# Weight preparation folded into an attention turn, the input fetched a turn earlier, tables for the edge turns, and zero-operand matmuls in TensorE's program

## The reference, cut to what matters

```
x -> attention   16 heads of width 8, twice: softmax(q k) v, and "lines" (exterior
                 products of w1,w2 with x, normalised) with geo_v; mixed by a gate
  -> FFN         activations and weights rounded to FP4 in blocks of 16, silu gate, 352 wide
  -> Mamba block RMS norm, 256 channels, causal conv of 4, 16 states scanned over 256 tokens
  -> FFN         512 wide, gelu; weights plus scale * outer products of tokens 1 to 16
```

## Time and profile before

| | us |
|---|---|
| median of 3 runs | 897.81 |
| the three runs | 893.03, 897.81, 901.17 |
| the profiled execution | 895.68 |
| its span, first to last instruction | 893.9 |
| PE busy, share of the span | 658.1, 74% |
| DVE busy | 626.8, 70% |
| ACT busy | 426.3, 48% |
| POOL busy | 350.5, 39% |
| mean granted TensorE clock | 0.859 |

### The profile page before, as it was taken

The page is one execution under the profiler, slowest core; times in us unless marked ns, Lnnn a source line. Parts: engine busy times, 40 slices in busy tenths (PEclk is TensorE's granted clock), DMA queues, the critical chain, the costliest instruction groups (busy, mean ns, idle before and its releaser), DMA issues.

```text
span 893.9 us, 12114 instructions
## 1 busy us (share of the span) xinstructions
PE 658.1 (74%) x3939; PEld 401.5 (45%) x3939; DVE 626.8 (70%) x1230; ACT 426.3 (48%) x896; POOL 350.5 (39%) x328
## 2 busy tenths in 40 slices
PE   3258763897769896898589858978698678866355
PEld 2134442554545464446444545546444454444124
DVE  1826167697868786887779785978698859754671
ACT  1212532682549344854377345825483438433522
POOL 5513131492219512653348223932184007300640
PEclk9995976898889968997889887997899879967695
DMA  5221300341034201430134003410242005000400
GB/s 135 72 76 44 104 9 28 113 161 47 1 122 141 89 0 50 165 136 0 48 120 182 1 19 126 152 54 0 74 168 104 0 16 167 24 1 6 164 25 7
DMA packets 40447, 65.99 MB, mean 74 GB/s; under 512 B 7281, under 2 KB 29634, under 8 KB 38082
## 3 DMA queue, kind: packets, MB, share of 16 engines
q1 hardware_dynamic: 38242, 64.57, 21.7%
q10 hardware_dynamic: 2176, 1.05, 0.4%
HBM read 57.68 MB, written 7.86 MB: 73 GB/s over the span
## 4 chain that ended last, share of the span: by engine, by line
PE 49%; DVE 31%; issue 9%; ACT 6%; DMA 3%; POOL 1%; SPq 0%; DVEq 0%; POOLq 0%
PE ps_s L1036 14%; PE ps_v L1036 10%; PE ps_f L1036 9%; PE ps_y L1036 7%; PE ps_n L1036 6%; DVE shared L997 5%; DVE mx L897 4%; DMA x_tm<-in_L_attn_x_dram 2%; DVE bn L821 1%; DVE x L834 1%; PE ps_f L1040 1%; DVE shared L1002 1%; DVE qamax L790 1%; ACT L602 1%; DVE z L942 1%
## 5 line engine op out<-in xcount | busy, mean ns | idle before, releaser
L581 POOL TENSOR_TENSOR shared<-u,bcrow 128x1024 f32<-128x1024 f32 x64 | 199.3, 3119 | 125.3 <-DVE u L986 79.9
L997 DVE TENSOR_TENSOR_SCAN shared<-ps_f,shared 128x512 f32<-128x512 f32 x128 | 151.6, 1212 | 26.9 <-POOL shared L581 15.5
L897 DVE TENSOR_REDUCE mx<-ps_s 128x2 f32<-128x512 f32 (+1 forms) x192 | 127.3, 686 | 55.5 <-PE ps_s L1036 54.6
L1036 PE MATMUL ps_s<-stack_mem 72*128 72x128 bf16 (+3 forms) x1024 | 152.7, 270 | 7.5 <-DVE mx L897 6.5
L1036 PE MATMUL ps_y<-shared,ident 128*128 128x512 f32 x256 | 124.8, 615 | 30.2 <-DVE shared L1002 30.1
L752 ACT ACTIVATE ps_f<-delta,amat 128x255 f32<-128x255 f32 x256 | 111.0, 476 | 39.0 <-DVE shared L997 22.8
L1036 PEld LDWEIGHTS ps_s<-stack_mem 74*128 74x128 bf16 (+1 forms) x1024 | 87.6, 106 | 67.1 <-issue 24.2
L669 ACT ACTIVATE probs<-ps_s 128x512 f32<-128x512 f32 x192 | 104.9, 597 | 21.8 <-PE ps_s L1036 21.2
L1036 PEld LDWEIGHTS ps_y<-shared,ident 128*128 128x128 f32 x256 | 44.5, 192 | 80.2 <-DVE shared L1002 44.2
L1002 DVE TENSOR_TENSOR shared<-shared,bcrow 128x1024 f32<-128x1024 f32 x64 | 78.4, 1225 | 2.2
L1036 PE MATMUL ps_s<-causal,ident_bf 128*128 128x256 bf16 (+1 forms) x192 | 67.4, 354 | 6.3 <-DMA stack_mem<-stack_dram 4.3
(11 more groups left out here) (205 smaller groups left out, 1038.4 us busy)
## 6 DMA issues: line engine op xcount, KB each, us to landing
bcrow<-bc_dram SPq DMA_DIRECT2D x64, 512.0 KB, 4.0
stack_mem<-stack_dram SPq DMA_DIRECT2D x96, 192.0 KB
stack_dram<-parts SPq DMA_DIRECT2D x24, 256.0 KB, 2.5
x_tm<-in_L_attn_x_dram ACTq DMA_DIRECT2D x8, 128.0 KB, 6.0
xb<-in_L_attn_x_dram SPq DMA_DIRECT2D x8, 128.0 KB, 2.2
out_dram<-y_out SPq DMA_DIRECT2D x8, 128.0 KB, 2.4
fmem<-in_L_attn_conv_w_dram SPq DMA_DIRECT2D x1, 512.0 KB
lmem<-in_L_ffn_W_dram SPq DMA_DIRECT2D x2, 256.0 KB
```

The costliest lines, as they stand in the source:

```text
L581: G.tensor_tensor(bx[:, j % 2], u[:].unsqueeze(2).to_broadcast(S4), bcrow[:, j % RING, 0].unsqueeze(1).to_broadcast(S4), ALU.mult).then_in ...
L897: V.tensor_reduce(mx[:, a, min(i, 1), hd[0]:hd[-1] + 1:2], ps_s[:, n % 2].rearrange("p (h n) -> p h n", h=len(hd)), AX.X, ALU.max).then_in ...
L997: V.tensor_tensor_scan(hs[:, j % HB, c].rearrange("p n t -> p (n t)"), ps_f[:, c, :], bx[:, j % 2, c].rearrange("p n t -> p (n t)"), 0.0, ...
L1036: return nc.tensor.matmul(o, lhsT, rhs, start=start, stop=stop, **kw)
```

## The change

Four things are edited. `setup` becomes a generator whose steps are merged into turn -1 with `prep(1)` and `core(0)`; on PE the transposes of W1 and W2 now come first and those of the quantized weights last, and the waits for the prepared weights move to their first users in turn 0. ACT starts the transfer of x for batch f+1 right after it has copied the transposed x of batch f. `EDGE` gives turns -1, 0, 7 and 8 tables of their own (turn 5 leaves the hardware loop), while PLAN is changed in a few numbers. And a new stream `warm` puts 12 steps into PE's turns 0 to 7, each with two matmuls of a zero 128x128 bf16 weight with 512 moving columns into ps_y. A warm step that falls while ps_y sums up states accumulates zeros; the others overwrite a bank that has been read.

```
+WARM = 12
 PLAN "pe":
-        "prep": [0.9, 2.8, 3.9, 5, 6.6, 9.2, 25.8],
+        "prep": [0.9, 2.8, 3.9, 5, 6.6, 8.3, 24.1],
+        "warm": [1.5, 9.5, 11, 31, 33.5, 39.5, 40.5, 41.5, 42.5, 53.5, 61.5, 88],
+EDGE = {
+    -1: { ...
+        "pe": {
+            "prep": [0, 8.3, 14, 16, 18, 18.7, 26.3],
+            "setup": [0.8, 6.6, 9.8],
+            "core": [18.9, 19.8, 20.7, 22, ...
+    0: { ...
+            "ffn": [10.6, 12.3, 18.8, 19.9, 32.9, 36.6],
+            "warm": [19.6, 19.7, 19.8, 31, 33.5, 39.5, 40.5, 41.5, 42.5, 53.5, 61.5, 88],
...
             def turn(k):
...
+                plan = (EDGE.get(k, PLAN) if isinstance(k, int) else PLAN)[name]
+                interleave([(plan[stream.__name__], stream(k + ahead)) for stream, ahead in streams
+                            if stream.__name__ in plan and (not isinstance(k, int) or 0 <= k + ahead < BATCH)]
+                           + [(plan["setup"], setup()) for _ in range(1) if setup and isinstance(k, int) and k == -1])
...
             def prep(f):                                  # ACT
-                yield
-                if not is_first(f):
-                    act.wait_ge(xT_ps, f)
-                act.dma_start(x_tm[:], x[f].rearrange("(t p) n -> p t n", p=P)).then_inc(x_loaded, 16)
+                if is_first(f):
+                    act.dma_start(x_tm[:], x[f].rearrange("(t p) n -> p t n", p=P)).then_inc(x_loaded, 16)
                 yield
                 act.wait_ge(xT_ps, f + 1)
                 A(xT[:, 1:1 + T], ps_v[:, 0:T], ACT.Copy).then_inc(xT_sb, 1)
+                if not isinstance(f, int) or f < BATCH - 1:
+                    act.dma_start(x_tm[:], x[f + 1].rearrange("(t p) n -> p t n", p=P)).then_inc(x_loaded, 16)
...
             def setup():                                  # PE
+                yield
                 pe.wait_ge(s_w, ALL_W)
+                for c in range(RC):
+                    last = tr(ps_n[:, c * P:(c + 1) * P], w1_raw[:, c])
+                last.then_inc(s_pe0, 1)
+                yield
+                pe.wait_ge(s_act0, 2)
+                for c in range(RC):
+                    last = tr(ps_n[:, c * P:(c + 1) * P], w2_raw[:, c * P:(c + 1) * P])
+                last.then_inc(s_pe0, 1)
+                yield
                 pe.wait_ge(s_dve0, 3)
...
             def prep(f):                                  # PE
                 pe.wait_ge(x_loaded, f * 16 + 16)
+                if not is_first(f):
+                    pe.wait_ge(vals_all, f)
...
+            def warm(b):
+                for _ in range(WARM):
+                    yield
+                    if is_first(b):
+                        pe.wait_ge(xqT_sb, 1)
+                    else:
+                        pe.wait_ge(yg_sb, b)
+                    for _ in range(2):
+                        mm(ps_y[:], zero_bf[:], ident_bf[:].unsqueeze(1).to_broadcast([P, 4, P]),
+                           start=not summing[0], stop=not summing[0])
```

More of the change, by code:

```diff
@@ L61 @@
         "mamba": [49.1, 51.3, 57.3, 62.2, 63.8],
[L62 removed]
+        "scan": [67.4, 69, 71.4, 75.5, 78, 79.2, 81.7, 82.9, 85.7, 86.5, 89, 92.1, 94.5, 94.6, 97.3, 98.5],
     },
@@ L362, in turn @@
                     chain.restart()
-                interleave([(PLAN[name][stream.__name__], stream(k + ahead)) for stream, ahead in streams
-                            if stream.__name__ in PLAN[name] and (not isinstance(k, int) or 0 <= k + ahead < BATCH)])
-            turn(-2)
-            if setup:
-                setup()
-            turn(-1)
-            turn(0)
-            with eng.Fori(1, BATCH - 2) as k:
+                plan = (EDGE.get(k, PLAN) if isinstance(k, int) else PLAN)[name]
+                interleave([(plan[stream.__name__], stream(k + ahead)) for stream, ahead in streams
+                            if stream.__name__ in plan and (not isinstance(k, int) or 0 <= k + ahead < BATCH)]
+                           + [(plan["setup"], setup()) for _ in range(1) if setup and isinstance(k, int) and k == -1])
+            for k in range(-2, 1):
                 turn(k)
-            for k in range(BATCH - 2, BATCH + 1):
+            with eng.Fori(1, BATCH - 3) as k:
+                turn(k)
+            for k in range(BATCH - 3, BATCH + 1):
                 turn(k)
@@ L475, in _ @@
             G = nc.gpsimd
-            for t_, v in ((ident, 0.0), (causal, 0.0), (causalT, 0.0), (xT, 0.0), (linesn, 0.0)):
+            for t_, v in ((zero_bf, 0.0), (ident, 0.0), (causal, 0.0), (causalT, 0.0), (xT, 0.0), (linesn, 0.0)):
                 last = G.memset(t_[:], v)
@@ L1229, in ffn @@
                 pe.wait_ge(xq_sb, b + 1)
-                if not is_first(b):
+                if is_first(b):
+                    pe.wait_ge(s_act0, 4)
+                    pe.wait_ge(s_dve0, 4)
+                else:
                     pe.wait_ge(hs_sb, b * 16)
@@ L1339, in lora_ffn @@
                 last.then_inc(f1_ps, 1)
-            run(pe, None, "pe", ((prep, 2), (core, 1), (norm_std, 1), (norm, 0), (ffn, 0), (mamba, 0), (scan, 0), (scan_late, -1),
+            run(pe, None, "pe", ((prep, 2), (core, 1), (norm_std, 1), (norm, 0), (ffn, 0), (mamba, 0), (scan, 0), (scan_late, -1), (warm, 0),
                                  (mamba_out, -1), (lora_ffn, -1)), setup)
```

189 lines of the change are left out of this document (161 added, 28 removed), and 6 rows, old and new, of the table EDGE.

## The result

The changed kernel takes 887.56 us (median of 4 runs, 886.33 to 891.15), the kernel before, run beside it, 896.13 (893.03 to 901.17). The ratio is 0.990 with a 95% interval of 0.986 to 0.993: 1.0% faster, where 2.3% was forecast. The profiled execution took 886.33 us (span 884.5) against 895.68: 9.35 us gained of 20.

What follows compares the result with a forecast made beforehand. PE was taken as the main bound (49% of the chain, DVE 31%), slowed by low clock and waits. Turn -1 -12, turn 0 -4 and turns 1 to 6 -4 gave -20 us, about 877; range 860 to 893.

Steps and rivals of the forecast that it cites:

- Against this, the maps of `prep(2)` leave the path behind: Turn 0: offset to some 2 us of reordered work and 1.3 to 2.5 us of warm matmuls; sum -4 us.
- The small shifts in PLAN: 0: Loop turns: the changed order numbers were priced at 0, within 1 us for the sum of turns.
- steps 1 to 3: Warm steps by x's and x3's transposes: step 1 costs 0.14 us, the other two 0.88 high or 1.7 low.
- first fall: Clock drop near 408.9 us, ahead of the warm steps: stays, but a sooner rise returns 0.9 us.
- step 9: Warm step behind the transposes of the Mamba input: costs about 0.5 us.
- second fall: Clock drop near 439.6 us, ahead of the conv: three steps in the wait return 1.2 us, at an even chance.
- third fall: Clock drop near 456.7 us, at three units: one step nearly suffices; 1.9 us at 75% returns 1.4.
- step 11: Warm step in the run of exponential units where PE never pauses: costs 0.44 to 0.84 us.
- Rival 2: Loop turns: warm steps hold the clock up in most of a turn, -46 us in all, 852 us; chance 0.12.
- Rival 1: Warm steps return nothing, as zeros may not count or waits are too long; about 890 to 903 us; chance 0.15.
- Rival 3: Turn -1 gains only the wait for x, as DVE or `prep(1)` holds core(0); 885 us; chance 0.09.
- Rival 4: Turns 1 to 7: on-path warm steps paid in full at the low clock, 5 us a turn, 917 us; chance 0.06.

Runs made afterwards that it cites:

- e5: Kernel before with only the early x, the split setup and the table of turn -1; PLAN of before, no warm steps: 877.68 us.
- e11: Kernel before with only the request for x moved a turn ahead: 885.85 us.
- e10: e4 without the warm steps: 883.55 us.
- e4: Changed kernel with the table of turn -1 only; turns 0, 7 and 8 go by PLAN, turn 0 with its own first three warm times: 883.13 us.
- e1: Changed kernel without its twelve warm steps: 892.84 us, ratio 0.996 to the kernel before.
- e12: e5 with sixteen warm steps in waits (three before the first map of v, ten before the Mamba input, three among the last score units): 859.42 us.
- e6: e4 with warm steps 2 and 3 moved into the wait ahead of the first map of v, except in turn 0: 883.66 us.
- e14: e12 without the ten steps in the Mamba wait, so six steps remain: 878.02 us.
- e8: e4 with two small DVE writes, 0.54 us a turn, behind the read of ps_y: 900.34 us, with one run of 881.17.
- e13: e12 with only its ten steps in the wait for the Mamba input: 867.03 us.
- e9: e5 with the change's twelve warm steps added: 889.28 us, nine runs from 882.65 to 898.45.
- e15: e4 with e12's sixteen steps in place of its twelve: 887.21 us.
- e7: e4 with the identity instead of zeros as the warm steps' weight: 882.84 us.

## Why the prediction was wrong, point by point

The table of stretches splits the 10.65 us between forecast and profile: turn -1 gave 1.0 more than said, turn 0 missed 6.1, turns 1 to 6 missed 5.1, turn 7 0.4.

**Turn -1: right.** First unit at 48.65 (49.1 forecast), last maxima at 72.06 (71.7 by the sum, 72 to 73 as the check), no wait for x_tm, -13.0 (-12). e5 has it too (turn -1 ends at 93.26), and e11 splits it: 6.3 us by the request of x alone (my bound for it was 5), the rest by the split setup and the table of turn -1.

**Turn 0: wrong, by 6.1 us, and this is the larger failure.** The gain at its start was more than forecast (the transposes of the FFN's input, 128.57 before, come at 108.75: 6.8 us beyond turn -1's 13.0). The step that failed is the sum that ends in "Against this, the maps of `prep(2)` leave the path behind": only two score units, the two maps and three warm steps were priced against it. What the table EDGE[0] and the changed PLAN do in the rest of the turn was put at nothing, without a reason. The lead of 19.8 us became 17.7 at the gated product (six warm matmuls, 1.29 us on the chain, within my 1.3 to 2.5), 14.7 at the quantized transposes (the stretched DVE operation, 2.69 for 0.89, and the maxima inside the quantization, 1.29), and 10.9 at y0. By the experiments the 9.0 us between e5's y0 (187.47) and the changed kernel's (196.48) are: changed PLAN 4.1 (e10), warm steps 1.8 (e4 against e10), turn 0's table 3.1 (e4). The split is rough: each y0 is good to about 1 us, and it depends on the order of the parts, for with turn 0's table in place the steps made y0 1.8 us earlier, not later (e1). The order's share, 4.1 and 3.1, stands clear of that; the steps' share does not. I had written "The small shifts in PLAN: 0" for the loop turns, where it held for the length of a turn (95.2 to 95.7 in e5 and 95.4 to 95.6 in e10, turns 3 to 5), and never asked what they did in turn 0. The earlier trace rows could not have told me of the stretch beside POOL; the trace before had one (DVE L797, 2.33 us, in the same quantization), and I did not read it.

**Loop turns: wrong, by 5.1 us, and a part that looks right is luck.** For turn 3, in us, the four pieces, with e1 splitting what was measured:

| piece of turn 3 | forecast | measured (after less before) | the steps (after less e1) | all else (e1 less before) |
|---|---|---|---|---|
| to the transposes of the Mamba input: steps 1 to 3, first fall | +0.1 to +0.9 | -0.20 | -0.34 | +0.14 |
| to `delta`: step 9 +0.5, second fall -1.2 | -0.7 | -0.81 | +0.11 | -0.92 |
| to the first sum into ps_y: third fall -1.4, step 11 +0.6 | -0.8 | **+1.28** | +0.24 | +1.04 |
| rest: step 12 | +0.1 | -0.05 | -0.01 | -0.04 |

The granted clock came out as said, 0.91 (0.88 to 0.92), and loop turns 1 to 5 at 95.4 to 95.7 stand just above the 94 to 95.5. The conv's fall is shortened in turns 1 to 5, not gone in half of them; in turn 6 it is as long as before.

Three steps of the prediction failed here.

The second fall was credited with 1.2 us for the steps. The piece did shrink as forecast, but in e1, with no step, it is already 0.92 us shorter, and adding the steps makes it 0.11 longer. The steps themselves took the conv from 4.59 us of the chain (e1) to 3.95, a return of 0.64, and step 9 cost 0.76, against 0.5 forecast.

"Third fall: PE was nearly busy enough there, and one step adds 0.44 us" was wrong: one step did not prevent the fall, the piece is at 0.67 before, in e1 and after. Step 11 then ran low, on the path, 0.85 us, and the units behind it took 1.81 us instead of e1's 2.25. Its net cost is 0.24 us, where 0.8 were to be gained. Where three steps did prevent the fall (clock 1.00 in e12), the piece is 8.62 us. So in the kernel before the fall had been worth 0.6 us (9.21 - 8.62), not the 1.9 that I reckoned: at the high clock PE is busy in 6.44 of the 8.62 us and waits for other engines in the rest.

"The small shifts in PLAN: 0" holds for the length of the turn and hides +1.04 us in the third piece against -0.92 in the second. e10, which has PLAN without steps, has both. What lengthens the third piece is that the low stretch lies later in it, over the units that follow one another without a pause; e1's own turn 1, with the low clock from 58.4 us on as before and not from 60.0, takes 9.36. Why it lies later is not shown.

In turns 3 to 5 the twelve steps thus returned nothing at all, where I had -0.7 us a turn; over turns 1 to 6 they returned 1.1 us (571.76 in e1, 570.69 with them), in one execution of each. A slip of my own besides: 875.7 and 2.1 are 877.8, and the forecast says 877.

**What the sum as such misses.** I added returns and costs as if what is saved in one place were kept. e6 saved 2.4 us at x3's transposes and had none of it 27 us later; e14 saved 1.5 and ended 1.0 behind; e8 added 0.54 and lost 3.4; in e13 one loop body took 95.08 and 92.06 us. In e6, e8 and e14 the trace shows a low stretch that moved on to the FFN's products in the first piece, where PE has work without pause; in e13 one more low stretch ahead of the Mamba wait. So each low stretch that is left is a trap for what is gained ahead of it, and in these traces small edits came out anywhere from +3 to -3 us a turn. In the order of e5, filling the widest wait gave the most (e13), and the other steps paid on top of it (e12 over e13) and not without it (e14).

Different programs also settle on the same length turn after turn: 95.57 to 95.59 in turn 3 of the changed kernel, e1, e4, e6 and e10; 98.99 to 99.00 in e8, e9 and e15. They differ by up to 24 added matmuls and by order. It is no law: e7, in e4's order, took 95.84, and e5 95.23. That the clock's changes, which stay at the same place in the turn to 0.1 us in turns 2 to 4 of the changed kernel and are 0.2 us later in turn 5, tie the turn's length to themselves is my reading; no run varies the turn's work finely enough to show it. Nor is it shown why e15 catches the FFN and e12 doesn't.

**The rivals.** Rival 2 (clock held up, turns 5 to 6 us shorter) had the right mechanism and was not reached by the change; e12 reaches 3.5 us a turn. Rival 1 (the steps return nothing) is what loop turns 3 to 5 show, not for its first reason: zeros count (e7). Its second reason, waits longer than the steps can bridge, holds: three steps left 4.12 of 4.86 us open, ten left 0.55. Rival 3 is out (turn -1). Rival 4 priced the steps at 5 us a turn; in e9's trace, of one of its slowest runs, they cost 3.5, in another order than the change's.

**The skill weighed again.** Filling one wait from 4.86 to 0.55 us raised the clock behind it from 0.81 to 1.00 (e12). The Trainium skill, TensorE: Matmul & The Clock Gate, Why this matters for your kernels, asks for short idle gaps; e13 agrees for the conv behind the wait (3.7 us, at the high clock, in every loop turn), and twelve steps of which three stood in that wait were not enough. The same page, Part 1, What's actually happening, puts the ramp penalty below 1% of a typical kernel's span. I had applied that to every fall of the clock; the falls here come again in each turn, and e12 against e5, which differs in nothing but fillers, takes 859.42 for 877.68 us, 2.1%.
